# Two shared expert units moved behind the routed tiles, one batch combined early, expert weights read in 4 KB pieces

## The reference

```
x = x + fp8_product(layernorm(x), ctx, mask)                    # layer 0, first half
t = layernorm(x)
shared = sum over 2 experts of  gelu(t @ Wsh_up[e]) @ Wsh_down[e]
probs = softmax(t @ W_router);  two best of 16 experts per token, gate = their probabilities
routed = sum over those 2 of    gate * (gelu(t @ Wrt_up[e]) @ Wrt_down[e])
x = x + shared + routed                                         # layer 0, second half
x = x + attention(layernorm(x), ctx)                            # layer 1, 16 heads of 128
x = x + hadamard_ffn(layernorm(x))                              # layer 1, 2048 wide
```

## Time and profile before

| | us |
|---|---|
| median of three runs | 2119.46 |
| profiled execution | 2115.32 |
| its span | 2113.7 |
| PE busy | 2002.0 |
| DVE busy | 1328.3 |
| POOL busy | 891.0 |
| ACT busy | 848.5 |
| clock granted to PE, mean | 0.987 |

### The profile page before, as it was taken

How to read it: one execution, slowest core, us unless ns; L and a number is a source line. 1 busy time by engine, 2 the same in 40 slices (tenths; PEclk the granted TensorE clock), 3 DMA queues, 4 the chain that set the end, 5 groups by cost and what they waited for, 6 DMA issues and landing times. The chain is left out here.

```text
span 2113.7 us, 28970 instructions
## 1 busy us (share of the span) xinstructions
PE 2002.0 (95%) x9797; PEld 1646.5 (78%) x9801; DVE 1328.3 (63%) x2087; ACT 848.5 (40%) x1649; POOL 891.0 (42%) x755
## 2 busy tenths in 40 slices
PE   4989999976999999999999999999979999999999
PEld 4766777755878888887888888888867888888887
DVE  7985688867687767668676666666665333333333
ACT  4543288863444445445444444444432111111111
POOL 1100033324776767666666656766641122201200
PEclk9999999998999999999999999999989999999999
DMA  7350299974666566666555555555520111100002
GB/s 286 125 190 25 93 356 379 388 268 145 189 178 186 164 194 172 182 181 185 150 160 163 163 157 149 159 158 160 176 86 15 30 30 30 30 0 30 0 1 80
DMA packets 160830, 307.17 MB, mean 145 GB/s; under 512 B 15648, under 2 KB 41120, under 8 KB 160736
## 3 DMA queue, kind: packets, MB, share of 16 engines
q1 hardware_dynamic: 144432, 251.67, 38.8%
q0 software_dynamic: 16304, 54.28, 7.9%
HBM read 210.73 MB, written 95.16 MB: 145 GB/s over the span
## 5 line engine op out<-in xcount | busy, mean ns | idle before, releaser
L1481 POOL TENSOR_TENSOR t_pT_lo<-t_pT_raw,t_pT_hi 128x512 fp32r<-128x512 f32 x256 | 328.3, 1302 | 212.9 <-ACT t_pT_hi L1597 211.3
L1707 DVE TENSOR_REDUCE t_sums<-t_score 128x1 f32<-128x512 f32 x256 | 169.5, 688 | 128.8 <-PE t_score L52 128.3
L2083 DVE TENSOR_TENSOR f_lin<-f_lin,f_silu 128x512 f32<-128x512 f32 x64 | 44.8, 700 | 290.5 <-PE f_lin L52 290.5
L1612 ACT ACTIVATE t_probs<-t_score,t_sums 128x512 f32<-128x512 f32 x256 | 175.0, 684 | 84.3 <-DVE t_sums L1707 69.0
L1697 DVE STREAM_TRANSPOSE t_blocks<-t_probs 128x512 f32<-128x512 f32 x256 | 172.8, 694 | 22.5 <-ACT t_probs L1612 22.5
L1689 DVE SCALAR_TENSOR_TENSOR x_res<-t_out,t_sums,x_res 128x512 f32<-128x512 f32 x256 | 179.5, 741 | 7.4 <-PE t_out L52 7.4
L1597 ACT ACTIVATE t_pT_hi<-t_pT_raw 128x512 fp32r<-128x512 f32 x256 | 159.8, 625 | 2.3 <-DMA t_pT_raw<-turned_blocks 2.3
L2044 ACT ACTIVATE f_silu<-f_gate 128x512 f32<-128x512 f32 x64 | 38.3, 598 | 299.3 <-PE f_gate L52 299.3
L769 POOL DMA_INDIRECT e_xg<-normalised_tokens,e_token x47 | 59.1, 1258 | 194.8 <-PE e_bank L1240 117.6
L1591 ACT ACTIVATE t_o_hi<-t_o 128x512 fp32r<-128x512 f32 x64 | 38.3, 598 | 218.0 <-PE t_o L52 218.0
L1577 ACT ACTIVATE t_k_hi<-t_score 128x512 fp32r<-128x512 f32 x64 | 38.3, 598 | 203.1 <-PE t_score L52 203.1
(11 more groups left out here) (350 smaller groups left out, 5964.1 us busy)
## 6 DMA issues: line engine op xcount, KB each, us to landing
turned_blocks<-t_blocks SPq DMA_DIRECT2D x256, 256.0 KB, 3.6
t_pT_raw<-turned_blocks SPq DMA_DIRECT2D x256, 256.0 KB, 4.2
e_up_raw<-in_L_ffn_Wrt_up_dram SPq DMA_DIRECT2D x47, 512.0 KB, 7.2
e_down_raw<-in_L_ffn_Wrt_down_dram SPq DMA_DIRECT2D x47, 512.0 KB, 6.7
outputs_by_expert<-e_y_out SPq DMA_DIRECT2D x47, 256.0 KB, 7.0
wq_raw<-in_L_xattn_Wq_dram POOLq DMA_DIRECT2D x32, 256.0 KB, 4.5
wk_raw<-in_L_xattn_Wk_dram POOLq DMA_DIRECT2D x32, 256.0 KB, 2.8
wv_raw<-in_L_xattn_Wv_dram POOLq DMA_DIRECT2D x16, 512.0 KB, 4.9
```

The lines of the kernel that those rows point to most:

```text
L1481: pool.tensor_tensor(pT_lo[:, q], pT_raw[:, q], f32(pT_hi[:, q]), ALU.subtract).then_inc(p_ready, 1)
L1612: act.activation(probs[:, t % 2, :], score_bank[t][:, :], ACT.Exp, bias=neg_max[:, t:t + 1], accum_out=inv[:, p, t:t + 1]).then_inc(exp_re ...
L1707: dve.tensor_reduce(neg_max[:, t:t + 1], score_bank[t][:, :], AX.X, ALU.max, negate=True).then_inc(max_ready, 1)
L2083: dve.tensor_tensor(lin_bank[k][:, :], lin_bank[k][:, :], silu[:, k, :], ALU.mult).then_inc(mid_done, 1)
```

## The change

1. `UNITS` stays 8, but the dense part runs only `DENSE` = 6 units. `turn_again(3)`, units 6 and 7 go out of it. The tokens of the last batch are transposed around the last routed tile (`last_turn`), and the two units run after it (`last_up`, `last_down`), with banks and buffers of their own. SP loads the two shared experts again as loads 47 and 48 of the routed ring.
2. POOL gathers batch 0's routed outputs in `experts_phase` after all stores have landed, into weight buffers that are free by then; DVE's `combine(j)` and `stats.finish(dve, 0, 1)` stand among the postponed units. `attention_phase` gathers and combines only batch 1 at its entry, and its first normalisation comes first.
3. Routed weights are read as `(p k) m -> p k m`: partition `p` takes `KD` (or `KE`) adjacent rows, one piece of 4 KB. So that the products still match, the transposes read every fourth feature of a token (`by_row`), and every second of `gmid`.

```diff
-            up_flat = Wrt_up.rearrange("e (k p) m -> e p k m", p=P)
-            down_flat = Wrt_down.rearrange("e (k p) m -> e p k m", p=P)
+            up_flat = Wrt_up.rearrange("e (p k) m -> e p k m", p=P)
+            down_flat = Wrt_down.rearrange("e (p k) m -> e p k m", p=P)
 ...
+                by_row = xg[:, n % XG_RING, :].rearrange("p (t k) -> p k t", k=KD)
                 for k in range(KD):
-                    ins = pe.transpose(xgT_bank[n % 2][:, k * P:(k + 1) * P], xg[:, n % XG_RING, k * P:(k + 1) * P],
-                                       ident[:, :])
+                    ins = pe.transpose(xgT_bank[n % 2][:, k * P:(k + 1) * P], by_row[:, k, :], ident[:, :])
```

PE's order at the end of the dense part, and after the routed tiles:

```diff
             down(2)
-            turn_again(3)
             up(4)
-            pe.wait_ge(again_ready, 2 * TB)
             down(3)
             up(5)
             down(4)
             find_tokens(0)
-            up(6)
             down(5)
-            up(7)
             find_tokens(1)
-            down(6)
-            down(7)
 ...
                 g_down(n)
+                if n == NSLOT - 2:
+                    last_turn(0)
+                    last_turn(1)
+            last_turn(2)
+            last_turn(3)
+            last_up(0)
+            last_up(1)
+            last_down(0)
+            last_down(1)
```

`last_down(e)` uses three banks and waits, tile by tile, for the add three tiles before. DVE's order, in the dense part, in the routed loop and behind it:

```diff
             mark_places(1)
-            low(6)
+            mark_tiles(1)
             add(5)
-            mark_tiles(1)
-            low(7)
-            add(6)
             number_tokens()
-            add(7)
 ...
+                split_up(n + 2)
+                split_down(n + 1)
+                if n == NSLOT - 2:
+                    last_turned(0)
+                    last_turned(1)
+            last_turned(2)
+            last_turned(3)
+            last_low(0)
+            split_down(NSLOT + 1)
+            combine(0)
+            combine(1)
+            last_low(1)
+            last_add(0, range(0, 2))
+            combine(2)
+            last_add(0, range(2, TB))
+            combine(3)
+            stats.finish(dve, 0, 1)
+            last_add(1, range(TB))
 ...
+            def combine(j):
+                dve.wait_ge(y_tile[j], 32)
+                for i in range(K_TOP):
+                    dve.scalar_tensor_tensor(out=x_res[:, j, :], in0=y_back[i][j // 2][:, j % 2, :], scalar=gate[i][:, j:j + 1],
+                                             in1=x_res[:, j, :], op0=ALU.mult, op1=ALU.add).then_inc(combined, 1)
+                    dve.wait_ge(combined, K_TOP * j + i + 1)
+                stats.read_tile(dve, j, j == TB - 1)
```

ACT does the same at its place: `split_up` and `split_down` of loads 47 and 48, `last_turned(j)`, and gelu and copy of `last_unit(e)`. POOL behind its last gather of tokens:

```diff
+            for i in range(Y_RING):
+                pool.wait_ge(y_stored[i], 16 * len(range(i, NSLOT, Y_RING)))
+            pool.wait_ge(up_ready, E_SH + NSLOT)
+            pool.wait_ge(down_ready, E_SH + NSLOT)
+            for n in range(TB):
+                for i in range(K_TOP):
+                    pool.indirect_dma_start(y_back[i][n // 2][:, n % 2, :], ...).then_inc(y_tile[n], 16)
```

The entry of `attention_phase` on DVE (PE and ACT follow the same order: first batch 0's transposes and query, then keys and values):

```diff
-            for n in "qkv":
+            def first_parts(n):
                 dve.wait_ge(w_hi_ready[n], 1)
                 dve.tensor_tensor(w_lo[n][:], w_raw[n][:], f32(w_hi[n][:]), ALU.subtract).then_inc(w_ready[n], 1)
+            dve.scalar_tensor_tensor(out=shift[:, :], ...).then_inc(shift_ready, 1)
+            first_parts("q")
+            ln.vector_lo(dve, 0, xT_hi, xT_lo, 0)
+            first_parts("k")
             ctx_lo(0)
             ctx_lo(1)
-            for t in range(TB):
-                combine_tile(0, t)
-            stats.finish(dve, 0, 1)
-            dve.scalar_tensor_tensor(out=shift[:, :], ...).then_inc(shift_ready, 1)
+            first_parts("v")
+            project_q(0)
+            combine_tile(0)
+            combine_tile(1)
             project_k(0)
             values(0, 0, 0, score_bank[3][:, :])
-            combine_tile(1, 0)
-            ln.vector_lo(dve, 0, xT_hi, xT_lo, 0)
-            for t in range(1, TB - 1):
-                combine_tile(1, t)
-            project_q(0)
-            combine_tile(1, TB - 1)
+            combine_tile(2)
+            combine_tile(3)
             stats.finish(dve, 1, 1)
             ln.vector_norm(dve, 1, 1)
```

More of the change, by code:

```diff
@@ L615, in experts_phase @@
         token = al.sb("token", [NSLOT], U32)
+        after = ExitStack()
+        ala = Alloc(nc, after, "e_last")
+        last_xT_hi, last_xT_lo = ala.sb("xT_hi", [KD, S], F32R), ala.sb("xT_lo", [KD, S], F32R)
+        last_mid_hi = ala.sb("mid_hi", [2, KE, S], F32R)
+        after.close()
         xn = al.sb("xn", [NT, D])
@@ L686, in experts_phase @@
         y_ready = al.sem("y_ready")
+        y_tile = [al.sem(f"y_tile{t}") for t in range(TB)]
+        combined = al.sem("combined")
         y_stored = [al.sem(f"y_stored{i}") for i in range(Y_RING)]
@@ L735, in _ @@
             for i in range(NSLOT - STORE_LAG, NSLOT):
+                if i + STORE_LAG < NSLOT + E_SH:
+                    load(i + STORE_LAG)
                 store(i)
@@ L1225, in _, with last_turn, last_up, last_down @@
             find_tokens(0)
-            up(6)
             down(5)
-            up(7)
             find_tokens(1)
-            down(6)
-            down(7)
+            def last_turn(j):
+                if j < 2:
+                    pe.wait_ge(*((xgT_ready, gmid_ready)[j], NSLOT - 1))
+                else:
+                    pe.wait_ge(again_ready, TB + j - 1)
+                for k in range(KD):
+                    ins = pe.transpose(last_turn_bank[j % 2][:, k * P:(k + 1) * P], xn[:, TB * (B - 1) + j, k * P:(k + 1) * P],
+                                       ident[:, :])
+                ins.then_inc(again_turned, 1)
+            def last_up(e):
+                r = (NSLOT + e) % 2
+                pe.wait_ge(up_ready, E_SH + NSLOT + e + 1)
+                if e == 0:
+                    pe.wait_ge(xgT_ready, NSLOT)
+                    pe.wait_ge(gmid_ready, NSLOT)
+                pe.wait_ge(again_ready, 2 * TB)
+                for k in range(KE):
+                    ks = slice(k * P, (k + 1) * P)
+                    three_pass(pe, last_up_bank[e][k][:, :], lambda c: up_hi[:, r, c, ks], lambda c: up_lo[:, r, c, ks],
+                               lambda c: last_xT_hi[:, c, :], lambda c: last_xT_lo[:, c, :], KD).then_inc(up_done, 1)
+            def last_down(e):
+                r = (NSLOT + e) % 2
+                pe.wait_ge(down_ready, E_SH + NSLOT + e + 1)
+                pe.wait_ge(mid_ready, (DENSE + e + 1) * KE)
+                if e == 0:
+                    pe.wait_ge(y_ready, NSLOT - 1)
+                    pe.wait_ge(midT_ready, NSLOT)
+                for j in range(TB):
+                    n = (DENSE + e) * TB + j
+                    if e > 0 or j > 2:
+                        pe.wait_ge(added, n - 2)
+                    ts = slice(j * P, (j + 1) * P)
+                    three_pass(pe, last_down_bank[n % 3][:, :], lambda k: last_mid_hi[:, e, k, ts],
+                               lambda k: last_mid_lo[:, e, k, ts], lambda k: down_hi[:, r, k, :],
+                               lambda k: down_lo[:, r, k, :], KE).then_inc(down_done, 1)
             def turn(n):
@@ L1513, in group @@
                 if known(g) and g == 0:
-                    pool.wait_ge(combined, 3 * 2 * TB)
+                    pool.wait_ge(combined, 2 * 2 * TB)
                     gather(3, y_later)
@@ L1786, in combine @@
                 if i == 1:
-                    dve.wait_ge(combined, 2 * TB * b + TB)
+                    dve.wait_ge(combined, 2 * TB * (b - 1) + TB)
                 for t in range(TB):
```

144 lines of the change are left out of this document (93 added, 51 removed).

## The result

| | before | after |
|---|---|---|
| median, us | 2118.94 (15 runs) | 2114.31 (15 runs) |
| profiled execution, us | 2115.32 | 2115.52 |
| its span, us | 2113.7 | 2113.9 |

The ratio is 0.9979, 95% interval 0.9969 to 0.9989: 4.4 us faster (2.3 to 6.6), where 11 were forecast. The sign was right, the size was not.

A forecast was written before the change was run, and what follows sets the result against it. PE, 95% busy, was taken to bound the kernel and DMA its routed loop; -18.8 + 2 - 10 + 1.5 + 14.7 = -10.6 us gave 2108 us, 8 times in 10 between 2095 and 2122.

The forecast's parts named there:

- What bounds the kernel: Whole kernel: PE busy 95% of the span, so only its idle or slow-clock stretches, or less PE work, can be won.
- So DMA bounds this loop: Routed loop: DMA at share 1.05 and 382 GB/s sets the 4.13 us period, with PE 0.56 us behind.
- Part 1: Dense part loses two units: first routed transpose at 243.9 instead of 262.65 us, -18.8 us.
- The term for the clock: First routed tiles: after PE's idle stretch, 4 to 6 us of work at half speed, +2 us (bounds 0 and +4).
- Part 2: Routed loop, 4 KB pieces: period from 4.13 to 3.88 us over 40 tiles, -10 us (bounds 0 and -22).
- The stride: PE's transposes loading every fourth or second float: taken as nothing; above, a doubling, +0.14 us each.
- rival (a): Strided loads cost: PE replaces DMA as the loop's bound, 2122 us, or about 2135 with all six doubled; chance 0.17.
- its cover of 0.31 us: Routed loop: 3.88 - 3.57 us a tile, PE time that the DMA bound was to hide.
- Rival (b): Size of the weights' pieces does not matter in the routed loop: sum -0.6, 2119 us; chance 0.13.
- Rival (c): DMA stops bounding the routed loop: 3.57 us a tile, -22 in place of -10, about 2097 us; chance 0.13.
- Parts 3 to 5: Routed loop's end +1.5 us; postponed units with batch 0's combine (28.0 later) and attention's entry (13.3 shorter), together +14.7.
- The sum: All terms up to batch 1's normalisation in attention's entry: -10.6 us, 2108 us for the median.

The follow-up runs named there:

- l3: Kernel before (1 and 2 KB pieces) with only STORE_LAG 5 instead of 6, each store issued one load earlier: 2107.53 us, ratio 0.9954 to before.
- e5: Changed kernel, but SP issues the fifth load of routed weights only when the first gather has landed: 2110.76 us, ratio 0.9969 to before.
- e4: Changed kernel with each find_tokens moved ahead of down(4) and down(5), DVE's marks among unit 4's adds: 2106.25 us, ratio 0.9945 to before.
- e1: Kernel before with only the 4 KB pieces and the strided transposes: 2112.13 us, ratio 0.9975 to before.
- l1: Changed kernel with STORE_LAG 5 instead of 6, each store issued one load earlier: 2104.03 us, ratio 0.9935 to before.
- g3: Kernel before with 4 KB pieces, strided transposes and STORE_LAG 5, order of units untouched: 2102.02 us, ratio 0.9927 to before.
- e3b: Changed kernel with 1 and 2 KB pieces but still strided transposes (products of other pairs, same work): 2119.65 us, ratio 1.0011 to before.
- e2: Changed kernel with 1 and 2 KB pieces and transposes of adjacent features put back: 2118.34 us, ratio 1.0012 to before.
- l2: Changed kernel with STORE_LAG 5 and transposes of adjacent features, DVE and ACT writing features in the pieces' order: 2104.99 us, ratio 0.9944 to before.
- y4: Changed kernel with STORE_LAG 5, unstrided transposes and a fourth y_out buffer: 2104.79 us, ratio 0.9943 to before.
- c1: Changed kernel with STORE_LAG 5 and the earlier token list (find_tokens ahead of down(4) and down(5)): 2095.28 us, ratio 0.9893 to before.
- e3: Changed kernel with 4 KB pieces but transposes of adjacent features (products of other pairs, same work): 2114.79 us, ratio 0.9989 to before.

## Why the prediction was right or wrong

**What bounds the kernel.** That only idle and slow stretches of PE can be won held. The step that failed is the one from "So DMA bounds this loop" to a loop that "goes from 4.13 to 3.88 us". The division 1.573 MB/382 GB/s = 4.12 us was no evidence for it: a tile's traffic over the measured rate gives the period, whatever sets the period. What set it was the ring of three store buffers, which closed in every tile (5.2 us to the issue and 7.1 to the landing, 4.13 us a tile). The 4 KB pieces shortened the landing only from 7.1 to 6.8 us, and so the tile by 0.1 us, where the DMA with the chain loosened gave 0.21 to 0.26. The DMA was near its own bound as well, since l3 reaches only 392 GB/s and 4.03 us; two bounds lay 0.1 us apart, and I priced the release of one of them. I had the earlier trace rows in hand and put ACT's wait down as a consequence of full queues; I did not ask which store it was and when that had been issued.

**Part 1.** This is the second term that fell short. The wait in `down(5)` was there as worked out (1.96 us), and the order of DVE's marks set the list. The 3.6 us that are missing are three small things: `find_tokens(1)` began at 239.36, not 237.8, and issued in 1.5 us, not 0.8, PE's clock having fallen (0.66 on the mean between 236 and 241 us); the gather took 5.25 us, not 3.8, of which e5 gives 1.2 to the load beside it. I had written that the loads of the first four experts cost nothing, and had put no load beside the gather; the fifth stood there. The term for the clock, +2 for 1.4, held, and e4 shows that covering the gather with work takes it away.

**Part 2.** -10 was forecast, -4.1 measured (from the first to the 46th copy the five traces with late stores and 4 KB pieces take 180.0 to 183.8 us, the three with small pieces 184.1 to 186.7, on the mean 3.0 us apart; that of after is the shortest of its five, and e1 beside before gives only 1.4, so -4.1 is rather too much than too little). The price per tile, 0.25, was right (0.21 between l3 and l1, 0.26 between l3 and g3), and so was 3.88 as the DMA's own period (3.82); the chain gave out only half of it. By the overhead that the Trainium skill (DMA: Bandwidth & Descriptors, "Why small descriptors are slow") gives, I had estimated 4.5% of the weights' traffic, 0.12 us a tile; 0.21 to 0.26 were measured, about twice that.

**The stride**, taken as nothing, costs 0.06 us a load, all six of them. By rival (a)'s own sum that is past the point (0.05) at which PE leaves its cover of 0.31 us. But the 0.38 us that the six loads add are not "all exposed", as the prediction had it: PE's early tile went from 3.57 to 3.63 us, so 0.06 of them show. The 3.79 that the expectations of e1, e3b and l1 call PE's own period is no need of PE: in l1 the loads of the second transposes wait 0.22 us a tile for ACT's `e_gmid`, and ACT waits for the store. Rival (a) was thus right in the load and wrong in the effect: no kernel is shown slower by it (e3b against e2: 1.0011 and 1.0012; l1 against l2). The Trainium skill (SBUF — State Buffer, "Door 1: The DMA port swizzle") had a stride of 4 floats as free; the trace has 204 against 141 ns for a stride of four and 206 against 140 for a stride of two, so the distance within 16 bytes made no difference.

**Rival (b)**, that the pieces do not matter, is refuted by e1 (0.9975) and by 412 against 392 GB/s. **Rival (c)** had the right suspicion, "the store wait would vanish once the stores land sooner", but they landed hardly sooner in the changed kernel (6.8 against 7.1 us); and where the wait did vanish (y4) the loop stopped at 3.85, not at 3.57.

**Parts 3 to 5.** +1.5 and +14.7 were forecast, +1.4 and +14.6 measured, the attention's start 31.4 us behind the last copy (31.1). Over the twelve kernels with this order the way from the last copy to `shift` ran from 30.3 to 31.6 us and from there to the norm from 24.1 to 26.8 (together 54.6 to 58.4), with the same instructions; so the near perfect agreement is partly luck. PE's clock may be a part of it (the first matmul behind the 3.2 us wait took 0.50 us in some and 0.80 in others), which no run separates.

**The sum.** With the terms as measured it is -1.9 in the traces up to batch 1's norm; behind it, where the work is the same, after took 2.1 us more (span 2113.9 against 2113.7). The medians say -4.4. These differences are not located: they are of the size by which executions of one kernel differ (2106.9 to 2119.2 for after).

That the order of work alone costs 2.5 us (e2), since it uncovers the list and the gather, also means that it was worth making only with the list earlier: g3 and c1 both have the pieces and the early stores and differ by the order of work with e4's repair, and their ratios are 0.9927 and 0.9893, 7 us.

## What to carry to other kernels

When an engine waits for a transfer out of a ring, write the ring's equation (buffers x period = delay to the issue + landing) before calling the loop bandwidth bound: read the delay from the first tile, where it needs no counting. Traffic over the measured rate is no test, since it returns the period in any case. And the landing is no constant: here it grew from 6.8 to 10.0 us when the stores left earlier, so ask for the next bound as well. A transfer issued in program order behind other work's waits is late by that work's lag, and one more buffer or one step earlier in the queue is the cheap test. When work is taken out of a stretch, ask what it was covering: here two units had stood over a list and a gather, and putting other work there was worth more than the move itself.

## What the runs showed of the hardware

- A weight load of 128x128 float32 on PE took 141 ns from adjacent floats, 204 from every fourth and 206 from every second. DVE's 128x512 pass with such a read and permuted write took 782 ns against 579.
- Weights in 4 KB pieces beside gathers and stores moved 412 GB/s at a share of 1.03; in 1 and 2 KB pieces 392 at 1.06.
- A share of 1.02 to 1.05 did not prove the DMA full: releasing the stores' wait brought 2% (383 to 392 GB/s, before to l3) to 6% (390 to 412, e3 to l2) more throughput.
- A 256 KB store beside the loads and gathers landed 6.84 us after its issue on the mean at 398 GB/s (after), and 9.98 us at 412 (l1).
- SP's issue of a store, usually 0.42 to 0.48 us, took up to 1.6 us now and then in the loop; with small pieces and early stores (l3) 1.30 us was its median, at a share of 1.06, where before had 0.46 at 1.05. The stores of l3:
```profile
L728 SPq DMA_DIRECT2D outputs_by_expert<-e_y_out x34: 512/1302/2208, 286.6 to 419.5; - x34
```
